# Self-attention scores on two halves of TensorE's rows, in units of two blocks

## The chip, the cores and the metric

The kernel runs on one core of one Trainium2 chip, as one program. The metric is the device time of one execution in microseconds. Engines are named as in the profile: PE is TensorE, DVE VectorE, ACT ScalarE, POOL GpSimd, SP SyncE (here it only issues transfers).

## The reference, cut to what matters

Everything is fp32. An adapter block with 8 heads comes first, then a transformer block: self-attention, cross-attention and a gated feed-forward, each behind a layer norm and each added to x. The change is in self-attention, with 4 batches, 512 tokens, width 160, 20 heads of 64:

```python
DIM, HEADS, DHEAD = 160, 20, 64
q = jnp.einsum('bne,ef->bnf', x, wq).reshape(B, N, HEADS, DHEAD).transpose(0, 2, 1, 3)
k = jnp.einsum('bme,ef->bmf', ctx, wk).reshape(B, M, HEADS, DHEAD).transpose(0, 2, 1, 3)
v = jnp.einsum('bme,ef->bmf', ctx, wv).reshape(B, M, HEADS, DHEAD).transpose(0, 2, 1, 3)
scores = jnp.einsum('bhnd,bhmd->bhnm', q, k) * DHEAD ** (-0.5)
attn = jax.nn.softmax(scores, axis=-1)
out = jnp.einsum('bhnm,bhmd->bhnd', attn, v)
x = jnp.einsum('bnf,fe->bne', out.transpose(0, 2, 1, 3).reshape(B, N, HEADS * DHEAD), wo) + bo + x
```

In self-attention x and ctx are both the layer norm of x.

## The kernel before

The program runs `adapter`, `selfattn`, `crossattn` and `feedfwd` one after the other. In each, every engine has a queue of its own, written out in program order, and the engines meet only through semaphores. The change is in `selfattn`, and in the helpers of `Norm` that it calls.

`selfattn` works on pairs of heads, ten to a batch, as a pair fills 128 rows with its 2 x 64 columns of q and k. fp32 values are split in two parts, a rounded one (fp32r, "hi") and the rest ("lo"), and products are made of the parts. A projection of q or k is four matmuls of 512 columns (L202 to L205), one of v eight of 256 columns (L210 to L213). ScalarE rounds the result (`round_part`, L509, L512) and copies v (L516), VectorE makes the rest (`rest`, L586, L590).

The scores of one head have only 64 rows. So SyncE (`stack`) moves the parts with eight transfers a pair: `q_stack` holds hi over lo of one head on 128 rows, `k_stack` the same k part twice. Two matmuls (L416, L417) then give (q_hi + q_lo)(k_hi + k_lo), a block of 128 queries x 512 keys.

The loop runs over the 80 blocks n of a batch (a head has four, a pair eight). In slot n each engine does, in this order:

- TensorE: the scores of block n + 10 (`LEAD`), the value products of block n - 2 (`LAG`) for both heads of a pair, every second slot (L446), four transposes of the probabilities (`turns`, L427), and where `step_at` says so a projection of a later pair.
- ScalarE: the exponential of block n + 10 with its sum (`exps`, L524), every fourth slot the copy of transposed probabilities (`copy_turned`, L535), then `round_part` and `copy_att` (L530).
- VectorE: the row maxima of block n + 10 (`maxima`, L595), the reciprocal of the sum (`inverses`, L600), `copy_turned` in the other three slots (L605), then `rest`.
- GpSimd: the scaling of the probabilities by the reciprocal (`scale`, L665).

The scores have two banks, the transposed blocks two, the value products two (`b_out`, used by the output projection L454 as well), the projections two. `probs` has room for four heads: the first exponential of a head waits until the transposes of the head four before it are done. The copies of transposed blocks go to four buffers. In a batch, statistics of the next layer norm are made at slot 37, and it is turned (L157, L161) at slot 57 (`TURN_AT`), on the banks of the projections.

Of the kernel before, what the change touches and what calls it, by code (L numbers as in the profile page):

```python
# [19 lines left out]
F32 = mybir.dt.float32  # L20
F32R = mybir.dt.float32r
# [75 lines left out]
class Norm:  # L97
# [53 lines left out]

    def turn(self, pe, b, ident, banks, bank_free):

        pe.wait_ge(self.s_hat.sem, self.s_hat.at(self.before + b, QT - 1))
        bank_free(0)
        for q in range(QT):
            last = pe.transpose(banks[0][:, q * P:(q + 1) * P], self.hat[:, q, 0:P], ident[:])  # L157
        last.then_inc(self.s_turned.sem, 1)
        bank_free(1)
        for q in range(QT):  # L160
            last = pe.transpose(banks[1][0:DT, q * P:(q + 1) * P], self.hat[:, q, P:D], ident[:])  # L161
        last.then_inc(self.s_turned.sem, 1)

    def scale(self, act, b, banks):
# [4 lines left out]
        act.activation(self.full[:], banks[0], ACT.Identity, bias=self.shift[:, 0:1], scale=self.gain[:, 0:1]).then_inc(self.s_full.sem, 1)  # L169
        act.wait_ge(self.s_turned.sem, self.s_turned.at(self.before + b, 1))  # L170
        act.activation(self.full_tail[:], banks[1][0:DT, :], ACT.Identity, bias=self.shift[0:DT, 1:2], scale=self.gain[0:DT, 1:2]).then_inc(self.s_full.sem, 1)
# [79 lines left out]
def selfattn(nc, x, ident, ln, next_ln, w_q, w_k, w_v, w_o, bias_o, banks, next_w_q, raw):  # L251

    LEAD, LAG = 10, 2  # L260
    NB = H1 * QT
    PAIRB = 2 * QT
    V_BUF = (0, 1, 2, 0, 1)
    V_BEFORE = (3 - 5, 4 - 5, 2 - 5, 0, 1)
    PS = 4
    TS = 4
    LN_AT = 37
    TURN_AT = (NPAIR - 3) * PAIRB + 1

    PROJECT, ROUND, REST = (20, 19, 16), (19, 18, 15), (18, 17)
    START = {1: (1, 0), 2: (1, 1), 3: (1, 2), 8: (2, 0), 9: (2, 1)}

    def step_at(n, ahead):

        for what, a in enumerate(ahead):
            j, off = divmod(n + a, PAIRB)
            if off == 0:
                return j, what  # L280
        return None

    def product_of(n):

        return n // 2

    with ExitStack() as ctx:
        sb = lambda n, s, d=F32: ctx.enter_context(nc.sbuf_tensor("sa_" + n, s, d))
        sig = lambda n, per, credit=0, step=1: Signal(ctx, nc, "sa_" + n, per, credit, step)
        q_stack = sb("q_stack", [P, 2, 2, S], F32R)  # L290
        k_stack = sb("k_stack", [P, 2, 2, 2, S], F32R)
        q_parts = sb("q_parts", [P, 2, S], F32R)
        k_parts = sb("k_parts", [P, 2, S], F32R)
        v = sb("v", [P, 3, QT, 2 * P])
        probs = sb("probs", [P, PS, QT, S])
        turned = sb("turned", [P, TS, S])
        att = sb("att", [P, NPAIR, S])
        negmax = sb("negmax", [P, 4 * QT])
        total = sb("total", [P, 4 * QT])
        inverse = sb("inverse", [P, 4 * QT])  # L300

        b_scores, b_turn, b_out, b_proj = banks[0:2], banks[2:4], banks[4:6], banks[6:8]
# [9 lines left out]

        s_stack = [sig(f"stacked{i}", NPAIR // 2, 0, 8 * 16) for i in range(2)]
        s_scores = sig("scores_made", NB, 8 * QT)
        s_max = sig("max_made", NB)
        s_exp = sig("exp_made", NB, 4 * QT)
        s_inv = sig("inverse_made", NB)
        s_norm = sig("probs_scaled", NB)
        s_noted = ctx.enter_context(nc.semaphore("sa_inverse_noted"))
        s_noted_sp = ctx.enter_context(nc.semaphore("sa_parts_noted"))  # L320
        s_turn = sig("turned_made", NB, 4 * QT)
        s_evac = sig("turned_copied", NB * 3 // 4, 3)
        s_evac_act = sig("turned_copied_act", NB // 4, 1)
        s_pv = sig("pv_made", NB // 2, 6 * QT)
        s_att = sig("att_copied", NPAIR, 2)
        s_o = sig("out_projected", 2, 2)
        s_bias = sig("bias_added", 1)
        s_x = sig("x_updated", QT, QT)
# [7 lines left out]
        def wait_turned_copied(eng, b, n):  # L336
            g, k = divmod(n, 4)
            if k == 3:
                eng.wait_ge(s_evac_act.sem, s_evac_act.at(b, g))
            else:  # L340
                eng.wait_ge(s_evac.sem, s_evac.at(b, 3 * g + k))
# [3 lines left out]
        @block.sync  # L345
        def _(sp):
            def stack(b, j):

                s = j % 2
                places = [(e, slice(e * HD, (e + 1) * HD), half, slice(half * HD, (half + 1) * HD)) for e in range(2) for half in range(2)]  # L350
                sp.wait_ge(s_scores.sem, s_scores.at(b, PAIRB * (j - 1) - 1))
                sp.sem_inc(s_noted_sp, 1)
                sp.wait_ge(s_qlo.sem, s_qlo.at(b, j))
                for e, rows, half, to in places:
                    sp.dma_start(q_stack[to, s, e, :].bitcast(F32), q_parts[rows, half, :].bitcast(F32)).then_inc(s_stack[s].sem, 16)
                sp.sem_inc(s_noted_sp, 1)
                sp.wait_ge(s_klo.sem, s_klo.at(b, j))
                for e, rows, half, to in places:
                    sp.dma_start(k_stack[to, s, e, :, :].bitcast(F32), k_parts[rows, :, :].bitcast(F32)).then_inc(s_stack[s].sem, 16)

            for j in range(3):
                stack(0, j)

            def batch(b, more):
                for j in range(3, NPAIR):
                    stack(b, j)
                if more:
                    for j in range(3):
                        stack(b + 1, j)
                else:  # L370
                    sp.wait_ge(s_q.sem, s_q.at(b, NPAIR - 1))
                    w_q.load(sp, next_w_q, raw, s_next)

            over_batches(sp, batch)

        @block.tensor
        def _(pe):
# [3 lines left out]
            def turn_norm(norm, b, nb):  # L381

                def bank_free(i):

                    if i == 0:
                        pe.wait_ge(s_vsb.sem, s_vsb.at(b, -1))
                    else:
                        pe.wait_ge(s_klo.sem, s_klo.at(b, -1))
                norm.turn(pe, nb, ident, b_proj, bank_free)

            def project(b, j, what):
                if j == 0 and what == 0:
                    ln.ready(pe, b)
                if what == 0:
                    if j > 0:
                        pe.wait_ge(s_vsb.sem, s_vsb.at(b, j - 1))
                    ln.project(pe, b_proj[0], w_q, j * P).then_inc(s_q.sem, 1)
                elif what == 1:
                    if j > 0:
                        pe.wait_ge(s_klo.sem, s_klo.at(b, j - 1))  # L400
                    ln.project(pe, b_proj[1], w_k, j * P).then_inc(s_k.sem, 1)
                else:
                    pe.wait_ge(s_qlo.sem, s_qlo.at(b, j))
                    for t in range(2):
                        last = ln.project_tokens(pe, b_proj[0][:, t * 2 * P:(t + 1) * 2 * P], w_v, j // 2 * 2 * P, j % 2 * 2 + t, 2 * P)
                    last.then_inc(s_v.sem, 1)

            def scores(b, n):
                h, q = divmod(n, QT)
                j, e = divmod(h, 2)  # L410
                if n % PAIRB == 0:
                    pe.wait_ge(s_stack[j % 2].sem, s_stack[j % 2].at(b, j // 2))
                pe.wait_ge(s_exp.sem, s_exp.at(b, n - 2))
                lhs = q_stack[:, j % 2, e, q * P:(q + 1) * P]
                bank = b_scores[n % 2]
                pe.matmul(bank, lhs, k_stack[:, j % 2, e, 0, :], start=True, stop=False)  # L416
                pe.matmul(bank, lhs, k_stack[:, j % 2, e, 1, :], start=False, stop=True).then_inc(s_scores.sem, 1)  # L417

            def turns(b, n):
                j, i = divmod(n, PAIRB)  # L420
                k, e = divmod(i, 2)
                h = 2 * j + e
                if k == 0:
                    pe.wait_ge(s_norm.sem, s_norm.at(b, QT * h + QT - 1))
                wait_turned_copied(pe, b, n - 2)
                for q in range(QT):
                    last = pe.transpose(b_turn[n % 2][:, q * P:(q + 1) * P], probs[:, h % PS, q, k * P:(k + 1) * P], ident[:])  # L427
                last.then_inc(s_turn.sem, 1)

            def pv(b, n):  # L430

                j, i = divmod(n, PAIRB)
                k, e = divmod(i, 2)
                if e == 0:
                    return
                wait_turned_copied(pe, b, n - 1)
                wait_turned_copied(pe, b, n)
                if k == 0:
                    pe.wait_ge(s_vsb.sem, s_vsb.at(b, j | 1))
                    if j >= 2:  # L440
                        pe.wait_ge(s_att.sem, s_att.at(b, j - 2))
# [1305 lines left out]
```

## Time and profile before

| | |
|---|---|
| runs (3) | median 1209.48 us, 1207.38 to 1214.39 |
| profiled execution | span 1209.3 us |
| TensorE busy | 1143.5 us, 95% |
| VectorE, ScalarE, GpSimd busy | 748.8, 621.4, 355.7 us |
| self-attention | from about 213 to 888 us |
| mean granted TensorE clock | 0.983 |

The time of the program is its span with a little around it. Self-attention is over half of it. An engine's idle time matters only where the engine sets the end, so the rows are to be read by stretch and not by the shares of the whole.

### The profile page before, as it was taken

To read this page: it belongs to the slowest core of one execution; us is meant where nothing else is said; L and a number is where in the kernel's file an instruction comes from. 1 tells how busy PE (TensorE), PEld (TensorE's weight loads), DVE (VectorE), ACT (ScalarE), POOL (GpSimd) and SP (SyncE) were. 2 spreads that over 40 slices of the span, in tenths; PEclk is the share of its full clock that TensorE was granted. 3 is DMA by queue.
4 is the path that set the end of the run, shared out by engine and by line. 5 is a ranking of instruction groups with operands and counts; after the bars stand their busy time and mean duration, and the time that the engine had idled before them with its cause. 6 is when DMAs were issued, how large, how long until landed. Compare 5 with 4: busy or idle time off the path is not lost. (4 is left out here: it accounts for less than half of the span.)

```text
span 1209.3 us, 21134 instructions
## 1 busy us (share of the span) xinstructions
PE 1143.5 (95%) x6348; PEld 766.6 (63%) x6348; DVE 748.8 (62%) x1758; ACT 621.4 (51%) x1370; POOL 355.7 (29%) x470
## 2 busy tenths in 40 slices
PE   7999999599999899999999999999989999999898
PEld 3555555456666666657566567666577778786787
DVE  4374574377777377774777775777637575757253
ACT  2543444356566366663565663656516464646242
POOL 2330321233433133432334332333213131312110
PEclk9999999799999999999999999999989999999899
DMA  6500000444444244444244443445120000000000
GB/s 167 114 1 1 0 1 1 104 105 105 106 105 105 56 105 106 111 99 107 58 111 107 95 108 81 111 103 118 42 55 2 1 0 0 0 1 1 1 22 22
DMA packets 43427, 76.69 MB, mean 63 GB/s; under 512 B 13316, under 2 KB 21444, under 8 KB 43332
## 3 DMA queue, kind: packets, MB, share of 16 engines
q1 hardware_dynamic: 43332, 75.54, 27.0%
q8 instruction: 46, 0.75, 0.3%
q14 instruction: 49, 0.40, 0.1%
HBM read 11.29 MB, written 1.31 MB: 10 GB/s over the span
## 5 line engine op out<-in xcount | busy, mean ns | idle before, releaser
L524 ACT ACTIVATE sa_probs<-banks,sa_negmax 128x512 f32<-128x512 f32 x320 | 220.9, 690 | 268.1 <-DVE sa_negmax L595 267.5
L665 POOL TENSOR_SCALAR sa_probs<-sa_probs,sa_inverse 128x512 f32<-128x512 f32 x320 | 223.1, 698 | 418.6 <-DVE sa_inverse L600 418.6
L595 DVE TENSOR_REDUCE sa_negmax<-banks 128x1 f32<-128x512 f32 x320 | 219.5, 686 | 104.8 <-PE banks L417 104.6
L427 PEld LDWEIGHTS banks<-ident,sa_probs 128*128 128x128 f32 x1280 | 146.5, 140 | 150.1 <-issue 69.1
L605 DVE COPY sa_turned<-banks 128x512 f32<-128x512 f32 x240 | 162.8, 679 | 66.4 <-PE banks L427 66.0
L427 PE MATMUL banks<-ident,sa_probs 128*128 128x128 f32 x1280 | 200.1, 279 | 1.1 <-issue 1.1
L446 PE MATMUL banks<-sa_turned,sa_v 128*64 128x512 f32 x640 | 172.6, 617 | 3.0 <-ACT sa_turned L535 1.7
L416 PE MATMUL banks<-sa_k_stack,sa_q_stack 128*128 128x512 f32 x320 | 144.8, 453 | 19.3 <-DMA sa_k_stack<-sa_k_parts 8.2
L417 PE MATMUL banks<-sa_k_stack,sa_q_stack 128*128 128x512 f32 x320 | 127.8, 399 | 0.0
L1537 POOL TENSOR_TENSOR ca_probs<-ca_probs,ca_inverse 128x616 f32<-128x616 f32 x40 | 48.8, 1219 | 162.4 <-DVE ca_inverse L1485 162.4
L416 PEld LDWEIGHTS banks<-sa_k_stack,sa_q_stack 128*128 128x128 f32 x320 | 61.3, 192 | 28.8 <-ACT sa_probs L524 13.6
L1417 ACT COPY ca_turned<-banks 77x512 f32<-77x512 f32 x80 | 42.7, 583 | 71.6 <-PE banks L1350 71.6
L446 PEld LDWEIGHTS banks<-sa_turned,sa_v 128*64 128x64 f32 x640 | 31.8, 134 | 59.7 <-issue 50.2
L1341 PEld LDWEIGHTS banks<-ca_k_diag,ca_q 128*128 128x128 f32 x320 | 45.3, 197 | 34.3 <-DVE ca_v L1466 23.2
L417 PEld LDWEIGHTS banks<-sa_k_stack,sa_q_stack 128*128 128x128 f32 x320 | 61.8, 193 | 3.6
L524 ACT ACTIVATION_READ_ACCUMULATOR sa_probs<-banks,sa_negmax 128x1 f32 x320 | 62.6, 196 | 0.0
L1341 PE MATMUL banks<-ca_k_diag,ca_q 128*128 128x154 f32 x320 | 54.0, 314 | 5.4 <-DVE ca_v L1466 2.8
L535 ACT COPY sa_turned<-banks 128x512 f32<-128x512 f32 x80 | 46.2, 577 | 8.2 <-PE banks L427 8.2
L600 DVE RECIPROCAL sa_inverse<-sa_total 128x1 f32<-128x1 f32 x320 | 49.0, 153 | 0.4 <-ACT sa_probs L524 0.4
L1360 PE MATMUL banks<-ca_turned,ca_v 77*64 77x512 f32 x160 | 46.1, 634 | 2.3 <-ACT ca_turned L1417 2.3
L1370 PEld LDWEIGHTS banks<-w_o,ca_att 128*128 128x128 f32 x320 | 45.7, 198 | 4.0 <-issue 4.0
L202 PE MATMUL banks<-ln_y_hi,wa_hi 128*128 128x512 f32 x80 | 39.3, 491 | 8.5 <-issue 3.5
(189 smaller groups left out, 1992.2 us busy)
## 6 DMA issues: line engine op xcount, KB each, us to landing
sa_k_stack<-sa_k_parts SPq DMA_DIRECT2D x160, 256.0 KB, 4.2
sa_q_stack<-sa_q_parts SPq DMA_DIRECT2D x160, 128.0 KB, 2.3
w_o<-in_L_xattn_wo SPq DMA_DIRECT2D x2, 800.0 KB, 6.3
out<-x SPq DMA_DIRECT2D x4, 320.0 KB, 2.5
x<-in_x SPq DMA_DIRECT2D x1, 960.0 KB, 5.3
ad_raw_main<-in_L_xattn_wq SPq DMA_DIRECT2D x1, 640.0 KB, 4.6
ad_raw_main<-in_L_xattn_wk SPq DMA_DIRECT2D x1, 640.0 KB, 7.4
ad_raw_main<-in_L_xattn_wv SPq DMA_DIRECT2D x1, 640.0 KB, 10.0
```

Of the source, the lines that this page charges most:

```text
L416: pe.matmul(bank, lhs, k_stack[:, j % 2, e, 0, :], start=True, stop=False)
L417: pe.matmul(bank, lhs, k_stack[:, j % 2, e, 1, :], start=False, stop=True).then_inc(s_scores.sem, 1)
L427: last = pe.transpose(b_turn[n % 2][:, q * P:(q + 1) * P], probs[:, h % PS, q, k * P:(k + 1) * P], ident[:])
L446: last = pe.matmul(b_out[j % 2][e * HD:(e + 1) * HD, :], v[:, V_BUF[j // 2], k, c:c + HD], turned[:, (n - 1 + e) % TS, :], start=(k == 0), ...
L524: act.activation(probs[:, h % PS, q, :], b_scores[n % 2], ACT.Exp, bias=negmax[:, c:c + 1], accum_out=total[:, c:c + 1]).then_inc(s_exp.se ...
L535: act.copy(turned[:, n % TS, :], b_turn[n % 2]).then_inc(s_evac_act.sem, 1)
L595: dve.tensor_reduce(negmax[:, c:c + 1], b_scores[n % 2], AX_X, ALU.max, negate=True).then_inc(s_max.sem, 1)
L600: dve.reciprocal(inverse[:, c:c + 1], total[:, c:c + 1]).then_inc(s_inv.sem, 1)
L605: dve.tensor_copy(turned[:, n % TS, :], b_turn[n % 2]).then_inc(s_evac.sem, 1)
L665: pool.tensor_scalar(probs[:, h % PS, q, :], probs[:, h % PS, q, :], inverse[:, c:c + 1], 1.0, ALU.mult, ALU.mult).then_inc(s_norm.sem, 1)
L1341: last = pe.matmul(b_scores[:, q // 2, (q % 2) * 2 * SK:(q % 2 + 1) * 2 * SK], q_sb[:, j % BUFS, q * P:(q + 1) * P], k_diag[:, j % BUFS, : ...
L1537: pool.tensor_tensor(p, p, inverse[:, j % BUFS, :].unsqueeze(2).broadcast_to([P, 2 * QT, SK]), ALU.mult).then_inc(s_norm.sem, 1)
```

## The change

The two heads of a pair are taken together. `q_parts` and `k_parts` now have two buffers and stay as they are, head 0 on rows 0 to 63, head 1 on rows 64 to 127; the stacks, their semaphores and SyncE's transfers go. The scores of a unit (block q of both heads) are six matmuls with 64 rows each: for hi x hi, lo x hi and hi x lo one of each head, into two banks. lo x lo is left out. The loop has 40 units a batch, LEAD is 5, and the value products of unit u - 1 follow the scores of unit u + 5. Each unit has eight transposes in two groups, one for each head, each with its bank. `probs` has room for two pairs, the copies of transposed blocks for two units. ScalarE copies head 1 of odd units, VectorE all others. Maxima and reciprocals are made for both heads in one instruction; exponentials and scalings stay one for each head. The projections have one bank, the value products one, and the output projection writes the banks of the transposes. `part_at` puts the projections of pair j + 2 behind units 4j, 4j + 1 and 4j + 2. The layer norm of what follows is turned in two steps, after units 23 and 27.

```diff
-    LEAD, LAG = 10, 2
-    NB = H1 * QT
-    PAIRB = 2 * QT
+    NU = NPAIR * QT
+    LEAD = 5
...
+    LN_AT = 12
+    TURN_MAIN, TURN_TAIL, ROUND_AT = 23, 27, 31
+    START = {0: (1, 0), 1: (1, 1), 2: (1, 2)}
+    def part_at(u):
+
+        j, what = u // QT + 2, u % QT
+        return (j, what) if what < 3 else None
...
-        q_stack = sb("q_stack", [P, 2, 2, S], F32R)
-        k_stack = sb("k_stack", [P, 2, 2, 2, S], F32R)
-        q_parts = sb("q_parts", [P, 2, S], F32R)
-        k_parts = sb("k_parts", [P, 2, S], F32R)
+        q_parts = sb("q_parts", [P, 2, 2, S], F32R)
+        k_parts = sb("k_parts", [P, 2, 2, S], F32R)
-        probs = sb("probs", [P, PS, QT, S])
-        turned = sb("turned", [P, TS, S])
+        probs = sb("probs", [P, 2, 2, QT, S])
+        turned = sb("turned", [P, 2, 2, S])
...
-        b_scores, b_turn, b_out, b_proj = banks[0:2], banks[2:4], banks[4:6], banks[6:8]
+        b_scores, b_turn, b_out, b_proj = [banks.pair(0), banks.pair(2)], banks[4:6], banks[6], banks[7]
...
                 elif what == 1:
-                    if j > 0:
-                        pe.wait_ge(s_klo.sem, s_klo.at(b, j - 1))
-                    ln.project(pe, b_proj[1], w_k, j * P).then_inc(s_k.sem, 1)
+                    pe.wait_ge(s_qlo.sem, s_qlo.at(b, j))
+                    ln.project(pe, b_proj, w_k, j * P).then_inc(s_k.sem, 1)
...
+            def scores(b, u):
+
+                j, q = divmod(u, QT)
+                if q == 0:
+                    pe.wait_ge(s_klo.sem, s_klo.at(b, j))
+                pe.wait_ge(s_exp.sem, s_exp.at(b, 2 * u - 3))
+                bank = b_scores[u % 2]
+                for i, (a, c) in enumerate(((0, 0), (1, 0), (0, 1))):
+                    for e in range(2):
+                        rows = slice(e * HD, (e + 1) * HD)
+                        last = pe.matmul(bank[:, e, :], q_parts[rows, j % 2, a, q * P:(q + 1) * P], k_parts[rows, j % 2, c, :],
+                                         start=(i == 0), stop=(i == 2))
+                last.then_inc(s_scores.sem, 1)
...
+            def turns(b, u):
+
+                j, k = divmod(u, QT)
                 if k == 0:
+                    pe.wait_ge(s_norm.sem, s_norm.at(b, 2 * QT * j + 2 * QT - 1))
+                for e in range(2):
...
+                    wait_turned_copied(pe, b, u - 1, e)
+                    for q in range(QT):
+                        last = pe.transpose(b_turn[e][:, q * P:(q + 1) * P], probs[:, j % 2, e, q, k * P:(k + 1) * P], ident[:])
+                    last.then_inc(s_turn.sem, 1)
...
+                for u in range(NU):
+                    m = u + LEAD
+                    if m < NU:
                         scores(b, m)
                     elif more:
+                        scores(b + 1, m - NU)
+                    if u >= 1:
+                        pv(b, u - 1)
+                    turns(b, u)
...
+                    if u == TURN_MAIN:
+                        norm.turn_main(pe, nb, ident, b_proj, lambda: pe.wait_ge(s_vsb.sem, s_vsb.at(b, u // QT + 2)))
...
+                wait_turned_copied(pe, b, NU - 1, 0)
+                pe.wait_ge(s_att.sem, s_att.at(b, NPAIR - 2))
+                project_out(0, 0, NPAIR - 2)
+                pv(b, NU - 1)
...
+            def exps(b, u):
+                j, q = divmod(u, QT)
+                act.wait_ge(s_max.sem, s_max.at(b, u))
                 if q == 0:
+                    act.wait_ge(s_turn.sem, s_turn.at(b, 2 * QT * (j - 1) - 1))
+                for e in range(2):
+                    act.activation(probs[:, j % 2, e, q, :], b_scores[u % 2][:, e, :], ACT.Exp, bias=negmax[:, u % RING, e:e + 1],
+                                   accum_out=total[:, u % RING, e:e + 1]).then_inc(s_exp.sem, 1)
...
+            def copy_turned(b, u):
+                act.wait_ge(s_turn.sem, s_turn.at(b, 2 * u + 1))
+                act.wait_ge(s_pv.sem, s_pv.at(b, u - 2))
+                act.copy(turned[:, u % 2, 1, :], b_turn[1]).then_inc(s_evac_act.sem, 1)
...
+                    if u % QT == 0 and u > 0:
+                        copy_att(b, u // QT - 1)
+                    if u % 2 == 1:
+                        copy_turned(b, u)
...
+            def maxima(b, u):
+                dve.wait_ge(s_scores.sem, s_scores.at(b, u))
+                dve.tensor_reduce(negmax[:, u % RING, :], b_scores[u % 2], AX_X, ALU.max, negate=True).then_inc(s_max.sem, 1)
...
+                    copy_turned(b, u, 0)
+                    if u % 2 == 0:
+                        copy_turned(b, u, 1)
```

## Rows read from the trace of the kernel before

**Rows 1.** The page: busy us, share of the span and instructions of each engine.

```profile
PE 1143.5 (95%) x6348; PEld 766.6 (63%) x6348; DVE 748.8 (62%) x1758; ACT 621.4 (51%) x1370; POOL 355.7 (29%) x470
```

**Rows 2.** Busy time by stretch: stretch, length, engines (instructions), granted clock, DMA share, GB/s.

```profile
310.28:325.61 15.33, 15.00 (x83) 9.14 (x82) 12.92 (x37) 8.49 (x21) 6.27 (x10) 1.00 0.46 105
325.61:340.30 14.69, 14.69 (x83) 9.09 (x82) 10.64 (x25) 9.53 (x25) 7.52 (x10) 1.00 0.47 108
340.30:357.32 17.02, 16.02 (x91) 9.91 (x89) 12.37 (x27) 11.76 (x28) 5.93 (x8) 1.00 0.42 98
...
386.71:416.50 29.79, 26.66 (x163) 20.09 (x162) 11.64 (x29) 9.84 (x24) 5.54 (x8) 1.00 0.26 60
```

**Rows 3.** Timeline of TensorE in steady state: start, length (us), engine, line, tiles.

```profile
428.21 0.48 PE L416 MATMUL banks<-sa_k_stack,sa_q_stack 128*128 128x512 f32 x1
428.53 0.40 PE L417 MATMUL banks<-sa_k_stack,sa_q_stack 128*128 128x512 f32 x1
428.86 1.08 PE L446 MATMUL banks<-sa_turned,sa_v 128*64 128x512 f32 x4
429.87 0.66 PE L427 MATMUL banks<-ident,sa_probs 128*128 128x128 f32 x4
430.28 0.47 PE L416 MATMUL banks<-sa_k_stack,sa_q_stack 128*128 128x512 f32 x1
430.60 0.40 PE L417 MATMUL banks<-sa_k_stack,sa_q_stack 128*128 128x512 f32 x1
430.83 0.60 PE L427 MATMUL banks<-ident,sa_probs 128*128 128x128 f32 x4
431.19 0.47 PE L202 MATMUL banks<-ln_y_hi,wa_hi 128*128 128x512 f32 x1
...
432.19 0.40 PE L416 MATMUL banks<-sa_k_stack,sa_q_stack 128*128 128x512 f32 x1
```

**Rows 4.** Timeline of all engines, the same stretch.

```profile
422.44 0.68 DVE L586 SCALAR_TENSOR_TENSOR sa_q_parts<-banks,sa_q_parts 128x512 fp32r<-128x512 f32 x1
...
423.04 0.68 DVE L595 TENSOR_REDUCE sa_negmax<-banks 128x1 f32<-128x512 f32 x1
...
425.56 0.40 PE L417 MATMUL banks<-sa_k_stack,sa_q_stack 128*128 128x512 f32 x1
...
426.00 0.69 DVE L595 TENSOR_REDUCE sa_negmax<-banks 128x1 f32<-128x512 f32 x1 [0.36 <-PE banks L417]
...
426.72 0.69 ACT L524 ACTIVATE sa_probs<-banks,sa_negmax 128x512 f32<-128x512 f32 x1 [0.94 <-DVE sa_negmax L595]
...
433.77 0.66 PE L427 MATMUL banks<-ident,sa_probs 128*128 128x128 f32 x4
...
434.27 0.59 ACT L509 ACTIVATE sa_q_parts<-banks 128x512 fp32r<-128x512 f32 x1
434.46 0.69 DVE L605 COPY sa_turned<-banks 128x512 f32<-128x512 f32 x1 [0.83 <-PE banks L427]
```

**Rows 5.** Timeline, ScalarE near the start of self-attention.

```profile
245.38 0.69 ACT L524 ACTIVATE sa_probs<-banks,sa_negmax 128x512 f32<-128x512 f32 x1 [1.36 <-DVE sa_negmax L595]
...
246.06 0.68 ACT L524 ACTIVATE sa_probs<-banks,sa_negmax 128x512 f32<-128x512 f32 x1
```

**Rows 6.** Timeline near the end of self-attention.

```profile
870.82 0.59 ACT L535 COPY sa_turned<-banks 128x512 f32<-128x512 f32 x1 [4.35 <-PE banks L427]
...
871.55 1.08 PE L446 MATMUL banks<-sa_turned,sa_v 128*64 128x512 f32 x4 [0.33 <-ACT sa_turned L535]
...
874.09 1.08 PE L446 MATMUL banks<-sa_turned,sa_v 128*64 128x512 f32 x4 [0.44 <-DVE sa_turned L605]
```

**Rows 7.** Timeline of the first scores; in brackets the idle time before.

```profile
226.31 0.79 PE L416 MATMUL banks<-sa_k_stack,sa_q_stack 128*128 128x512 f32 x1 [8.21 <-DMA sa_k_stack<-sa_k_parts]
```

**Rows 8.** Timeline of VectorE, the statistics of the next layer norm.

```profile
314.17 0.99 DVE L131 BATCH_NORM_STATS2 ln_stats<-x 128x6 f32 x4
...
315.61 0.66 DVE L595 TENSOR_REDUCE sa_negmax<-banks 128x1 f32<-128x512 f32 x1
```

More of the change, by code:

```diff
@@ L251, in selfattn @@
 def selfattn(nc, x, ident, ln, next_ln, w_q, w_k, w_v, w_o, bias_o, banks, next_w_q, raw):
-    LEAD, LAG = 10, 2
-    NB = H1 * QT
-    PAIRB = 2 * QT
+    NU = NPAIR * QT
+    LEAD = 5
     V_BUF = (0, 1, 2, 0, 1)
     V_BEFORE = (3 - 5, 4 - 5, 2 - 5, 0, 1)
[L265 to L285, printed above, removed]
+    RING = 8
+    LN_AT = 12
[4 more added lines that the diff above has]
+        return (j, what) if what < 3 else None
     with ExitStack() as ctx:
@@ L346, in _ @@
         def _(sp):
[L347 to L374, printed above, removed]
+            sp.wait_ge(s_q.sem, s_q.at(B - 1, NPAIR - 1))
+            w_q.load(sp, next_w_q, raw, s_next)
         @block.tensor
@@ L444, in pv, with project_out @@
                 for e in range(2):
                     c = j % 2 * P + e * HD
-                    last = pe.matmul(b_out[j % 2][e * HD:(e + 1) * HD, :], v[:, V_BUF[j // 2], k, c:c + HD],
-                                     turned[:, (n - 1 + e) % TS, :], start=(k == 0), stop=(k == QT - 1))
+                    last = pe.matmul(b_out[e * HD:(e + 1) * HD, :], v[:, V_BUF[j // 2], k, c:c + HD],
+                                     turned[:, u % 2, e, :], start=(k == 0), stop=(k == QT - 1))
                 last.then_inc(s_pv.sem, 1)
-            def project_out(b, q, first, end):
+            def project_out(q, first, end):
@@ L478, in batch @@
+                    if u == TURN_MAIN + 1:
+                        pe.wait_ge(norm.s_full.sem, norm.s_full.at(norm.before + nb, 0))
+                    if u == TURN_TAIL + 1:
+                        pe.wait_ge(norm.s_full.sem, norm.s_full.at(norm.before + nb, 1))
+                    if part_at(u):
+                        j, what = part_at(u)
                         if j < NPAIR:
@@ L616, in _ @@
             for what in range(2):
                 rest(0, 0, what)
-            for n in range(LEAD):
-                if n in START and START[n][1] < 2:
-                    rest(0, *START[n])
-                maxima(0, n)
-                if n >= 1:
-                    inverses(0, n - 1)
+            for u in range(LEAD):
+                maxima(0, u)
+                if u in START and START[u][1] < 2:
+                    rest(0, *START[u])
+                if u >= 1:
+                    inverses(0, u - 1)
@@ L625, in batch @@
             def batch(b, more):
[L626 to L628 removed]
+                for u in range(NU):
+                    m = u + LEAD
+                    if m < NU:
                         maxima(b, m)
                     elif more:
[L631 to L632 removed]
+                        maxima(b + 1, m - NU)
+                    if m - 1 < NU:
                         inverses(b, m - 1)
```

304 lines of the change are left out of this document (121 added, 183 removed).

## The prediction

> **What bounds the kernel now.** I read the page first: TensorE is busy 95% of the span, VectorE 62% [rows 1]. Then the busy times by stretch, cut at the starts of query projections, which come once per pair of heads in self-attention. In steady state a pair takes 14.69 us, all of it busy TensorE, at the full clock [rows 2]. Once per batch a pair takes 17.02 us (the next layer norm is turned there), once 15.33 us (its statistics sit in VectorE's queue). The third view is TensorE's timeline [rows 3], from which each step is priced by start to start. One pass over two blocks is 2.98 us (428.21 to 431.19): a scores matmul 0.235; the value products 1.01, and 0.10 more for the scores matmul before them (0.33 for 0.23); four transposes 0.41 and 0.36, and 0.08 more for the matmul behind each (0.32 for 0.235), so 0.49 and 0.44. Sum: 4 x 0.235 + 0.10 + 1.01 + 0.49 + 0.44 = 2.98. A projection of q or k is 1.00 less that 0.08, so 0.92; v is taken at 0.96. A pair: 4 x 2.98 + 2.80 = 14.72, the 14.69 measured. So here only TensorE's own work counts, as long as nothing it waits for is late. The rest of the argument is what becomes late.
>
> **TensorE's own work.** A unit (two blocks) had four scores matmuls on 128 rows. It gets six on 64 rows, in three couples on the two halves of the array. No row shows couples on row halves. The nearest are the value products, couples on column halves: one fp32 product of 512 columns would be four passes of about 0.22, 0.9 alone, and two of them take 1.01 together [rows 3]. So I take 0.235 a couple, 0.705 a unit; bounds 0.235 (free) and 0.47 (one after the other). Entering the row halves is a change the old order didn't have at this place (transposes led into plain matmuls). Price: below, nothing; above, 0.3 (three times the 0.10 that the change before the value products costs); I take 0.15, that 0.10 and a little for the second half starting later. New unit: 0.15 + 0.705 + 0.10 + 1.01 + 0.49 + 0.44 = 2.90, 0.085 less than before. Over 160 units: **-13.6**.
>
> The Trainium skill, page TensorEngine Tiling (Array Packing), Tiling Modes, says that changing the tiling mode drains TensorE. The trace agrees (the 0.10 above); if that rule cost nothing here the total would be 1229.6 us (worked below), with it 1237.
>
> **The wait that appears.** probs now holds two pairs. `exps(b, u)` with u = 4j, the first of pair j, waits for the last transposes of pair j-2, those of unit 4j-5. It stands in slot 4j-5 of ScalarE's queue, and the two exponentials stand ahead of `copy_turned` of that same slot, whose odd unit ScalarE copies. TensorE's value products of unit 4j-5 need that copy, and now come one slot later with only one scores unit between (no projection follows a unit with u % 4 = 3). Before, the wait was there too, but the copy was one block further on and the products two. The chain from the start of the second four transposes: they end and release in 0.63 (0.60 long [rows 3], and 0.03 as 433.77 + 0.66 to 434.46 [rows 4]); two exponentials at 0.68 [rows 5] = 1.36; copy and wake-up 0.73 (870.82 to 871.55 [rows 6]). Sum 2.72. TensorE fills 0.44 + 0.15 + 0.705 + 0.10 = 1.40 of it. It stands idle 1.32 us in every fourth unit: nine times a batch, eight in the last (the batch's last unit is followed by the output projection): 35 x 1.32 = **+46.2**. This stall doesn't shrink when the scores get cheaper.
>
> **A second chain.** q's rest on VectorE stands ahead of the next unit's maxima. From the start of q's projection: last matmul ends 0.705 + 0.40 later, wake-up 0.04 (425.56 to 426.00 is 0.44 [rows 4]), rounding 0.59, 0.03, then the maxima 0.60 behind the rest (422.44 to 423.04). The maxima of two blocks: between 0.69 and 1.38, taken at twice that spacing of 0.60, and 0.05 of wake-up, 1.25. Two exponentials 1.36, copy 0.73. Sum 5.71. TensorE's own way there: 0.92 + 0.15 + 0.705 + 0.10 + 1.01 + 0.49 + 0.44 + 0.92 + 0.15 + 0.705 + 0.10 = 5.69. Just hidden: **0**. If the change of mode were free it would cost 0.32. So a pair becomes 2.72 + 1.01 + 0.49 for the stalled unit, and 3 x 3.82 + 0.04 for the others: 15.7 us.
>
> **The rest.** All are small against the wait.
> - The last layer-norm turn: split over units 23 and 27, both stalled ones, with copies in ScalarE's slack. The 17.02 - 14.69 = 2.33 goes four times: **-9.3**.
> - Statistics: 1.44 on VectorE (314.17 to 315.61 [rows 8]) at unit 12, where q's rest already makes maxima late, so about 1.4 shows in place of 15.33 - 14.69 = 0.64: **+3**.
> - Start: the 8.21 wait for the stacking transfers [rows 7] goes, but one bank now makes k wait for q's rounding and rest (0.59 + 0.69), v for k's, and scores for v: 3.7 comes back: **-4.5**. Elsewhere the stacking transfers are hidden, so their removal is worth nothing; SyncE's queue has nothing behind them.
> - Batch end: the output projection now writes the transposes' banks and first waits for VectorE's copy (0.69 + 0.69 + 0.14 = 1.52 after the transposes begin, against 0.93): 0.6 x 4 = **+2.4**. A batch end costs 29.79 [rows 2]; its other waits I leave as they are.
> - Last batch, no scores or projections left to cover: a unit was 2.54 (871.55 to 874.09 [rows 6]). Now with the copy between: 0.63 + 0.73 + 1.01 + 0.49 = 2.86 when ScalarE copies, 0.28 more when VectorE makes both copies (0.69 + 0.60 + 0.83 from the first transposes). 0.45 x 5, and 1.2 for the three units before: **+3.5**.
> - VectorE's merged maxima and reciprocals, GpSimd's scales, one att bank, one update per half: VectorE was 72% busy in the steady pair (10.64 of 14.69), so nothing.
>
> Sum: -13.6 + 46.2 - 9.3 + 3 - 4.5 + 2.4 + 3.5 = +27.7. The profiled execution has a span of 1209.3 and the median of the runs is 1209.48, the same within 0.2. Forecast **1237.0**.
>
> Bounds by the unknown price of entering the row halves. At 0: own work -37.6, wait 35 x 1.47 = +51.6, second chain 35 x 0.32 = +11.2, rest the same: +20.3, 1229.6. At 0.3: +10.4, +41.1, 0: +46.6, 1256. The other terms may be off by some 8 together. Own range 1222 to 1262.
>
> **Rivals.**
> - *The other side: the chain over ScalarE doesn't hold TensorE.* If the copy of the odd unit is there when TensorE comes to it, the 46.2 goes and the total is 1209.3 - 18.5 = 1191. It decides at a stall of under 0.35 per fourth unit, where the total passes below 1203.4. For it: TensorE never waited for this copy in the steady pair before. Against it: the order of the queue and four durations, each from a row. Chance 0.11.
> - *Part of it:* stall of a third to two thirds, 1203 to 1222. Chance 0.10.
> - Forecast, 1222 to 1262: chance 0.60.
>
> 0.5% (6 us) is about what a measurement of this kernel can tell from no change. Under 1203.4: the third rival and a little of the part case, 0.13; within 6 us: 0.08; slower: 0.79. The range that leaves out the serial rival and the third one is 1205 to 1285.
>
> **What would show it.** In the profile after, query projections 15.7 apart in steady state. TensorE idle about 1.3 us before the value products of every fourth unit, released by ScalarE's copy into turned, and that copy right behind two exponentials that were released by transposes. TensorE's busy share falls to about 90%. The six scores matmuls start in couples, and the value products follow the first couple by some 0.8; if 1.5, the couples are serial. No 8 us wait at the start. Wrong would be a steady pair under 15 us, or one whose idle time stands before the scores (then the exponentials or maxima are the bound, which I take to be hidden).

## The result and the profile after

| | before | after |
|---|---|---|
| median (4 runs each, side by side) | 1208.84 us | 1242.13 us |
| range | 1207.38 to 1214.39 | 1241.65 to 1246.96 |
| span of the profiled execution | 1209.3 us | 1239.8 us |
| self-attention, first projection to the next stage's first | 677.3 us (213.42 to 890.72) | 706.9 us (215.82 to 922.76) |

The ratio is 1.0278 (95% interval 1.0229 to 1.0326): slower. Of the 30.5 us more in the span, 29.6 are in self-attention. The rest is outside it: the stage is reached 2.4 us later, and what follows it is 1.5 us shorter.

The page after: busy time of the engines, which answers to [rows 1], then costly groups.

```profile
PE 1140.1 (92%) x6668; PEld 742.7 (60%) x6668; DVE 730.4 (59%) x1430; ACT 611.1 (49%) x1370; POOL 351.9 (28%) x470
...
L485 ACT ACTIVATE sa_probs<-banks,sa_negmax 128x512 f32<-128x512 f32 x320 | 217.2, 684 | 272.7 <-DVE sa_negmax L557 206.4
...
L557 DVE TENSOR_REDUCE sa_negmax<-banks 128x2 f32<-128x1024 f32 x160 | 194.9, 1218 | 52.9 <-PE banks L371 50.3
L398 PE MATMUL banks<-sa_turned,sa_v 128*64 128x512 f32 x640 | 172.6, 617 | 47.3 <-ACT sa_turned L496 44.1
...
L371 PE MATMUL banks<-sa_k_parts,sa_q_parts 64*128 64x512 f32 x960 | 156.0, 430 | 4.4 <-issue 2.7
```

TensorE is busy 3 us less, 92% of the span instead of 95%. The group of the value products (L398) carries the new idle time, 47.3 us, nearly all of it ended by ScalarE's copy into turned (L496). The scores (L371) hardly wait: 4.4 us.

TensorE's waits for those products: us in total, times, longest.

```profile
PE banks L398 <- ACT sa_turned L496: 44.1, 43, 1.3
...
PE banks L398 <- DVE sa_turned L566: 3.1, 3, 1.0
```

Busy time by stretch, in the columns of [rows 2]: the pair with the statistics, a pair with a layer-norm turn, a plain pair.

```profile
290.69:307.71 17.02, 14.69 (x91) 8.44 (x90) 12.49 (x29) 8.83 (x23) 6.79 (x11) 1.00 0.00 0
323.44:339.17 15.73, 15.05 (x95) 8.87 (x94) 10.23 (x17) 9.03 (x22) 5.09 (x8) 1.00 0.01 2
431.46:447.20 15.74, 14.62 (x91) 8.45 (x90) 10.21 (x17) 8.80 (x23) 5.47 (x8) 1.00 0.00 1
```

A plain pair is 15.74 (15.71 to 15.74 in the first three batches, mean 15.72; 15.87 to 15.89 in the last) where it was 14.69. The pair with the turn has 15.05 of busy TensorE in 15.73, so the turn sits in idle time; before it took 17.02 [rows 2].

Timeline of one stalled unit after, TensorE and ScalarE.

```profile
442.23 1.10 PE L385 MATMUL banks<-ident,sa_probs 128*128 128x128 f32 x8
...
443.26 0.96 PE L371 MATMUL banks<-sa_k_parts,sa_q_parts 64*128 64x512 f32 x6
443.37 0.69 ACT L485 ACTIVATE sa_probs<-banks,sa_negmax 128x512 f32<-128x512 f32 x1 [1.89 <-PE banks L385]
...
444.05 0.68 ACT L485 ACTIVATE sa_probs<-banks,sa_negmax 128x512 f32<-128x512 f32 x1
...
444.71 0.58 ACT L496 COPY sa_turned<-banks 128x512 f32<-128x512 f32 x1
...
445.34 1.08 PE L398 MATMUL banks<-sa_turned,sa_v 128*64 128x512 f32 x4 [1.12 <-ACT sa_turned L496]
...
446.35 1.09 PE L385 MATMUL banks<-ident,sa_probs 128*128 128x128 f32 x8
...
447.20 0.47 PE L218 MATMUL banks<-ln_y_hi,wa_hi 128*128 128x512 f32 x1
```

The reader is to follow ScalarE. Transposes end and release the exponential at 443.37. It needed their place in probs, and ScalarE had stood idle for 1.89 before it. Two exponentials run, and only then the copy at 444.71, whose transposed blocks had been ready as long as the exponential had. TensorE has done its six scores matmuls and stands 1.12 before the value products, which start as soon as the copy ends.

### The profile page after: what moved, and what is told of

It reads as the page before. It is cut to its first block and busy times, and to the rows that moved or that the text cites. A ratio compares the mean times of both kernels' runs of the same rounds, so it can differ in the third digit from the quotient of the medians.

```text
span 1239.8 us, 20399 instructions
## 1 busy us (share of the span) xinstructions
PE 1140.1 (92%) x6668; PEld 742.7 (60%) x6668; DVE 730.4 (59%) x1430; ACT 611.1 (49%) x1370; POOL 351.9 (28%) x470
## 5 line engine op out<-in xcount | busy, mean ns | idle before, releaser
L557 DVE TENSOR_REDUCE sa_negmax<-banks 128x2 f32<-128x1024 f32 x160 | 194.9, 1218 | 52.9 <-PE banks L371 50.3
L398 PE MATMUL banks<-sa_turned,sa_v 128*64 128x512 f32 x640 | 172.6, 617 | 47.3 <-ACT sa_turned L496 44.1
L385 PEld LDWEIGHTS banks<-ident,sa_probs 128*128 128x128 f32 x1280 | 137.9, 141 | 129.1 <-issue 125.1
L566 DVE COPY sa_turned<-banks 128x512 f32<-128x512 f32 x240 | 157.3, 683 | 72.6 <-PE banks L385 71.9
L385 PE MATMUL banks<-ident,sa_probs 128*128 128x128 f32 x1280 | 175.7, 280 | 1.0 <-POOL sa_probs L626 1.0
L371 PE MATMUL banks<-sa_k_parts,sa_q_parts 64*128 64x512 f32 x960 | 156.0, 430 | 4.4 <-issue 2.7
L371 PEld LDWEIGHTS banks<-sa_k_parts,sa_q_parts 64*128 64x128 f32 x960 | 79.0, 187 | 54.1 <-issue 32.3
L398 PEld LDWEIGHTS banks<-sa_turned,sa_v 128*64 128x64 f32 x640 | 32.1, 134 | 106.9 <-ACT sa_turned L496 54.4
L553 DVE TENSOR_TENSOR sa_k_parts<-banks,sa_k_parts 128x512 fp32r<-128x512 f32 x40 | 27.7, 692 | 70.8 <-ACT sa_k_parts L473 70.8
L1302 PEld LDWEIGHTS banks<-ca_k_diag,ca_q 128*128 128x128 f32 x320 | 44.1, 192 | 34.6 <-DVE ca_v L1427 23.3
L496 ACT COPY sa_turned<-banks 128x512 f32<-128x512 f32 x80 | 46.7, 584 | 10.8 <-PE banks L385 10.8
L1331 PEld LDWEIGHTS banks<-w_o,ca_att 128*128 128x128 f32 x320 | 46.2, 199 | 4.0 <-issue 4.0
L405 PEld LDWEIGHTS banks<-w_o,sa_att 128*128 128x128 f32 x320 | 43.7, 190 | 5.8 <-issue 3.2
L1331 PE MATMUL banks<-w_o,ca_att 128*128 128x160 f32 x320 | 47.2, 311 | 0.0
L405 PE MATMUL banks<-w_o,sa_att 128*128 128x160 f32 x320 | 45.6, 302 | 1.6 <-DVE sa_turned L566 1.6
```

The lines of the kernel that those rows point to most:

```text
L371: last = pe.matmul(bank[:, e, :], q_parts[rows, j % 2, a, q * P:(q + 1) * P], k_parts[rows, j % 2, c, :], start=(i == 0), stop=(i == 2))
L385: last = pe.transpose(b_turn[e][:, q * P:(q + 1) * P], probs[:, j % 2, e, q, k * P:(k + 1) * P], ident[:])
L398: last = pe.matmul(b_out[e * HD:(e + 1) * HD, :], v[:, V_BUF[j // 2], k, c:c + HD], turned[:, u % 2, e, :], start=(k == 0), stop=(k == QT ...
L405: last = pe.matmul(b_turn[q // 2][:, q % 2 * D:(q % 2 + 1) * D], att[:, j, q * P:(q + 1) * P], w_o[:, j, :], start=(j == 0), stop=(j == NP ...
L496: act.copy(turned[:, u % 2, 1, :], b_turn[1]).then_inc(s_evac_act.sem, 1)
L557: dve.tensor_reduce(negmax[:, u % RING, :], b_scores[u % 2], AX_X, ALU.max, negate=True).then_inc(s_max.sem, 1)
```

## The experiments

All pair times are start to start of query projections. Times of the stage, self-attention, are from its first projection to the next stage's first, in the profiled execution. The first four kernels start from the changed kernel, the next three (head_by_head, dummy_transfers, statistics_moved) from copy_first, the last three from statistics_moved.

**1. The copy ahead of the exponentials, in the fourth unit alone.**

```diff
+                    if u % QT == 3:
+                        copy_turned(b, u)
                     (the exponentials of unit u + LEAD)
...
-                    if u % 2 == 1:
+                    if u % QT == 1:
```

> In every unit with u % 4 = 3, ScalarE copies the transposed block before its two exponentials, not after. Theory (the exponentials that wait for the same unit's transposes hold the copy): the 1.12 us idle before the value products of each fourth unit goes, a steady pair falls from 15.72 to 14.6 us, and the total by 36 x 1.12 = 40 to about 1202, some 0.6% under the kernel before. Rival (scores on row halves and their change of mode are what costs, the idle time only moves): the pair stays above 15.3 and the total above 1225.

Measured: 1206.52 us beside 1210.24 before, ratio 0.9959 (0.9937 to 0.9980). The span falls from 1239.8 to 1208.6. The same unit in its timeline:

```profile
437.33 1.10 PE L385 MATMUL banks<-ident,sa_probs 128*128 128x128 f32 x8
...
438.35 0.96 PE L371 MATMUL banks<-sa_k_parts,sa_q_parts 64*128 64x512 f32 x6
438.53 0.59 ACT L496 COPY sa_turned<-banks 128x512 f32<-128x512 f32 x1 [1.92 <-PE banks L385]
439.02 0.69 ACT L485 ACTIVATE sa_probs<-banks,sa_negmax 128x512 f32<-128x512 f32 x1
...
439.25 1.08 PE L398 MATMUL banks<-sa_turned,sa_v 128*64 128x512 f32 x4
```

The copy now starts 1.20 after the transposes begin and not 2.48, the exponentials wait behind it, and the value products follow the scores with no idle time. From the transposes to the value products it is 1.92 where it was 3.11 (442.23 to 445.34). So the place of one instruction in a queue held all of the loss and more: the theory stands. Two stretches of it, a plain pair and the one with the statistics:

```profile
277.81:292.36 14.55, 14.55 (x92) 8.45 (x90) 10.18 (x17) 8.70 (x23) 5.47 (x9) 1.00 0.01 2
292.36:308.25 15.89, 14.61 (x91) 8.43 (x90) 12.50 (x29) 8.69 (x23) 6.66 (x11) 1.00 0.00 0
```

The pair is 14.55, all TensorE. What the idle time had hidden comes back: 14.97 in the two pairs with a turn, 15.69 in the pair with the layer norm's remainder (two subtractions on VectorE). That is why the total is 1206.5 and not the 1202 expected: the stage is 34.6 us shorter (706.9 to 672.4), not 40, as 8 x 0.42 + 3 x 1.14 = 6.8 us reappear.

**2. ScalarE copies head 1 of even units instead of odd ones.** No copy of ScalarE then stands in the slot of the late exponentials.

```diff
-                    if u % 2 == 1:
+                    if u % 2 == 0:
                         copy_turned(b, u)
```

> ScalarE copies head 1 of even units, VectorE all other blocks. Theory: in the fourth unit VectorE does both copies and the products wait 0.3 instead of 1.12; but in the unit behind which v is projected the copy comes after late exponentials, 0.4 of new idle time. A pair 15.25, the total down by 17 to about 1225. Rival (any copy there is as late, since TensorE is simply ahead): no change, 1242.

Measured: 1224.84, ratio 1.0098 (1.0070 to 1.0127). Plain pairs are 14.88 to 14.90, those with a turn 15.11 and 15.33, those with the statistics or the remainder about 16.3. The 44.1 us of waits for ScalarE's copy fall to 14.5 in 29 waits, and 6.3 in 7 come for VectorE's, which now makes both copies of odd units one after the other. This is between the two orders. The total is the one expected, but the sizes are not: in a plain pair the two waits are 0.14 for VectorE (expected 0.3) and 0.27 for ScalarE (expected 0.4), which is better than the 15.25 forecast for a pair, and the pairs with other work, up to 16.30, make up for it.

**3 and 4. Two products and four products instead of three.** The first leaves hi x lo out of the scores, the second adds lo x lo.

```diff
-                for i, (a, c) in enumerate(((0, 0), (1, 0), (0, 1))):
+                for i, (a, c) in enumerate(((0, 0), (1, 0))):
```

```diff
+                for i, (a, c) in enumerate(((0, 0), (1, 0), (0, 1), (1, 1))):
```

> The product hi x lo is left out of the scores (two couples of matmuls a unit, not three). Theory (two chains over VectorE and ScalarE bound the units they end in): only one of the four units of a pair gets shorter by the full 0.23, a pair 15.5, span down by some 9 us. Rival (TensorE's own work bounds all units): 0.23 x 160 = 37 us less.

> The product lo x lo is added (four couples a unit). Theory: the stalled unit takes the couple into its idle time, the other three grow by 0.235, a pair 16.4, span up by about 29 us. Rival (couples one after the other, or every unit bound by TensorE): 0.235 x 160 = 38 us or, if serial, 75.

Measured, one execution each: spans 1231.2 (8.6 less) and 1268.8 (29.0 more). The spans aren't clean, since in both a few us of the stage ran at a lower granted clock (0.83 from 634 to 644 with two products, 0.79 from 417 to 425 and 0.69 from 598 to 609 with four). The plain pairs, all at 1.00, are 15.31 to 15.39 and 16.43, beside 15.72. A couple is 0.235 in each of four units, 0.94 a pair. Adding it costs 0.71, three times 0.235: the stalled unit takes it for nothing. Taking it away gives back 0.33 to 0.41 only, and the waits for the copy grow from 44.1 to 64.3 us. That is the sign of a chain over another engine: less work on TensorE mostly makes its idle time longer.

**5. The six matmuls in the order of heads**, all three of head 0 and then all three of head 1.

```diff
-                for i, (a, c) in enumerate(((0, 0), (1, 0), (0, 1))):
-                    for e in range(2):
+                for e in range(2):
+                    for i, (a, c) in enumerate(((0, 0), (1, 0), (0, 1))):
```

> The kernel with the copy first (span 1208.6 us, steady pair 14.55 us, TensorE never idle in it), and in each unit the three products of head 0 come before the three of head 1. Theory (the couples share the array's time, and TensorE keeps its order): only the third product of head 0 and the first of head 1 overlap, five steps of 0.235 in place of three, 0.47 more in every unit, a pair 16.4, span up by 75 us. Rival (the two row halves don't overlap in either order, 0.15 a matmul is what 64 rows cost): no change.

Measured, one execution: 1207.64, span 1205.6, pair 14.57. Nothing is lost, and the expectation fails. The rival on record, no overlap in either order, gives the same number. The start times within one unit, in ns, of the changed kernel and of this one, are both in couples:

```
couples in program order:   432574 432577 | 432908 432911 | 433144 433147
head by head:               432706 432716 | 433043 433053 | 433279 433289
```

The records don't name the rows, so which matmul is which is inferred. Two of the same half don't start together (0.23 to 0.34 apart in experiment 9, which also rules out the rival), so each couple here must be one of each half: TensorE starts matmuls of the free row half past those that wait for the busy one. The order in the program doesn't matter here.

**6. Eight dummy transfers a pair**, as large as the stacking ones, waited for by nobody but SyncE and its counting.

> The kernel with the copy first, and SyncE issues for each pair eight transfers of the old sizes and shapes, from the output weights to tiles that nobody reads. Theory (the stacking transfers were hidden in steady state, and share nothing with the engines that sets the end): no change, 1206.5, a pair 14.55. Rival (they took bandwidth from the engines' reads): some 0.1 us or more a pair, 1211 or above.

Measured: 1206.79, ratio 0.9964 (0.9939 to 0.9988), pair 14.55. A stretch of it:

```profile
430.00:446.00 16.00, 16.00 (x98) 8.79 (x94) 11.12 (x18) 9.47 (x25) 5.90 (x9) 1.00 0.52 118
```

DMA is at 0.52 and 118 GB/s, as in the same window of the kernel before (0.52, 120), and TensorE is never idle. The transfers that the change removes were hidden in steady state. At the start of self-attention they weren't, there TensorE waited for the first ones [rows 7].

**7. The statistics moved** from slot 12 to 14, and the two steps that follow them from 14 and 16 to 18 and 20.

```diff
-    LN_AT = 12
+    LN_AT = 14
...
-                    if u == LN_AT + 2:
+                    if u == LN_AT + 4:
...
-                    if more and u == LN_AT + 4:
+                    if more and u == LN_AT + 6:
```

> The kernel with the copy first, and the statistics and the standardizing of the next layer norm move from units 12 and 14 to units 14 and 18, both behind VectorE's copies where no rest of q or k is made, and where ScalarE's exponentials wait for transposes anyway. Theory: the pair with the statistics falls from 15.9 to 14.6, four times, so 5 us less: 1201. Rival (1.4 us of VectorE work shows wherever it stands): no change.

Measured: 1197.65 (1196.14 to 1201.17) beside 1210.97 before, ratio 0.9898 (0.9879 to 0.9916). The pair that was 15.89 and the one with the remainder:

```profile
284.90:299.46 14.56, 14.56 (x91) 8.45 (x90) 11.24 (x25) 8.71 (x23) 6.16 (x10) 1.00 0.00 0
358.50:374.19 15.69, 14.70 (x92) 8.48 (x90) 10.86 (x19) 9.19 (x23) 5.71 (x9) 1.00 0.00 0
```

The pair with the statistics takes no longer than a plain one now, and the stage is 5.5 us shorter than in copy_first (666.9 for 672.4), the 5 expected. The medians differ by 8.9. The rest isn't this edit's doing as far as the traces show: outside the stage the two kernels are the same, and the profiled executions had a mean granted clock of 0.987 here and 0.979 in copy_first. This version beats both kernels, the one before by 1.0% and the changed one by some 3.7% (0.9898 against 1.0278).

**8. The remainder on GpSimd**, in slot 30.

```diff
+                    if u == ROUND_AT - 1:
...
+                        pool.tensor_tensor(norm.lo[:], norm.full[:], norm.hi[:].bitcast(F32), ALU.subtract).then_inc(norm.s_lo.sem, 1)
```

> The kernel before this one (statistics moved), and the two subtractions of the next layer norm go from VectorE (unit 31) to GpSimd (unit 30). Theory: they hold VectorE's maxima of the next unit, and the pair of 15.68 falls to 14.6, four times: 4.4 us less than with the statistics moved alone, about 1197. Rival: the projection of the next batch waits for the rounding itself, and GpSimd's two operations are slower: no gain or a loss of 1 or 2 us.

Measured: 1201.32, ratio 0.9913 (0.9885 to 0.9940): no gain. The last pair falls to 14.55, but the one before it rises to 15.89. The timeline of GpSimd, and TensorE's transposes behind it:

```profile
362.03 1.27 POOL L656 TENSOR_TENSOR ln_y_lo<-ln_full,ln_y_hi 128x512 fp32r<-128x512 f32 x1 [0.93 <-ACT ln_y_hi L193]
363.45 1.27 POOL L659 TENSOR_TENSOR ln_y_tail<-ln_full_tail,ln_y_tail 32x512 fp32r<-32x512 f32 x1 [0.16 <-POOL ln_y_lo L656]
365.01 2.69 POOL L626 TENSOR_SCALAR sa_probs<-sa_probs,sa_inverse 128x512 f32<-128x512 f32 x4 [0.28 <-POOL ln_y_tail L659]
...
366.42 1.09 PE L385 MATMUL banks<-ident,sa_probs 128*128 128x128 f32 x8 [1.27 <-POOL sa_probs L626]
```

Two subtractions of 1.27 each make the scaling of a pair's last unit (35) late, and the pair's first transposes, which need all four units scaled, wait 1.27 for it. The number is the rival's. Of its reasons the slower operations hold, but what waits for them are the transposes and not the next batch's projection.

**9. All six matmuls on rows 0 to 63.** Both heads' scores are made from head 0's rows, so only the time is of use.

```diff
-                        rows = slice(e * HD, (e + 1) * HD)
+                        rows = slice(0, HD)
```

> The kernel with the copy first and the statistics moved, and the scores of head 1 are made from head 0's rows, so that all six matmuls lie on rows 0 to 63 and the output is not the reference's. Theory (what makes three couples cheap is that the two halves of the array work at once; the head-by-head order changed nothing because TensorE lets the halves run on independently): six steps of 0.235 in each unit, 0.70 more, a pair 17.4, span up by 113 us to about 1308. Rival (64 rows are simply faster, some 0.12 us a matmul wherever they lie): no change, 1195.

Measured, one execution: 1308.89, span 1306.9, pair 17.27, which is 2.72 more than 14.55 (0.68 a unit for the 0.70 expected). TensorE's timeline:

```profile
450.20 1.65 PE L371 MATMUL banks<-sa_k_parts,sa_q_parts 64*128 64x512 f32 x6
451.78 1.08 PE L398 MATMUL banks<-sa_turned,sa_v 128*64 128x512 f32 x4
452.79 1.09 PE L385 MATMUL banks<-ident,sa_probs 128*128 128x128 f32 x8
453.82 1.65 PE L371 MATMUL banks<-sa_k_parts,sa_q_parts 64*128 64x512 f32 x6
```

From the scores to the value products 1.58 (450.20 to 451.78), where it is 0.90: three steps of 0.23 more. A matmul on 64 rows takes as long (0.23) as one on 128 did [rows 3], and the couples are cheap only because the two halves run together.

**10. The remainder split over two slots of VectorE**, its first subtraction in slot 30, the second in 31.

```diff
+                    if u == ROUND_AT - 1:
...
+                        dve.tensor_tensor(norm.lo[:], norm.full[:], norm.hi[:].bitcast(F32), ALU.subtract).then_inc(norm.s_lo.sem, 1)
```

> The kernel with the copy first and the statistics moved, and the first of the next layer norm's two subtractions goes to the end of VectorE's unit 30, into the gap before the copy of unit 31, the second stays at unit 31. Theory: about 0.7 of the 1.13 us that the pair at unit 32 has over the others goes, four times, 1195 against 1197.7 for the kernel with both at unit 31. Rival (as on GpSimd: the earlier place holds something else): no change or a loss.

Measured: 1198.95, ratio 0.9910 (0.9877 to 0.9942): no gain. The two pairs are 15.39 and 14.78, 30.17 in place of 14.55 + 15.69 = 30.24. The rival holds: the first subtraction, at 358.93, makes VectorE's next maxima and its copy behind them late, and TensorE waits 0.45 for that copy (361.55) and 0.25 for the scalings (362.87).

## Why the prediction was right, step by step

Forecast 1237.0 (1205 to 1285, slower 0.79); measured 1242.13, and +30.5 of span, +29.6 of it in self-attention, against +27.7. The mechanism named is the one that copy_first removes. That the sum is so close is in part luck: own work was 8 us too favourable, and the wait (4 us) and the batch ends (about 1 us each) were too dear. The terms:

- **The wait that appears**, +46.2 = 35 x 1.32. Start to start a plain pair loses 15.72 - 14.55 = 1.17, by the order of the copy alone, and in the last batch 15.87 - 14.57 = 1.30; 27 x 1.17 + 8 x 1.30 = +42. The chain from the first of the eight transposes was put at 0.49 + 2.72 = 3.21 and is 3.11. The exponential starts 1.14 after them (1.12 taken), both take 1.34 (1.36), copy and wake-up 0.63 (0.73). TensorE's way meanwhile is 1.92 (1.89 taken). The 0.73 was read in the last batch of the kernel before [rows 6], and there it holds after as well: 819.43 to 820.16 below, where it is 0.64 in the stalled units of the first three batches. A price from one stretch was used for another.
- **Own work**, -13.6. This was mis-sized: 14.55 against 14.69 is 0.14 a pair, 40 x 0.14 = -5.6. A couple costs the 0.235 taken. Entering the row halves costs more. In the steady state after (timeline of TensorE below), the first couple starts 0.33 after the projection before it (432.24 to 432.57), 0.10 over 0.235, and scores take 0.89 to the value products (432.57 to 433.46), 0.08 over 0.705 + 0.10. That is 0.18 where 0.15 was taken; 4 x 0.03 = 0.12 a pair is 4.8 us of the 8 missing. Most of the rest is in my sums: 14.72 for the old pair's 14.69, and 14.52 with the measured price for the new one's 14.55, 0.06 x 40 = 2.4. The errors of this term (+8) and of the one above (-4) cancel by half.

```profile
432.24 0.40 PE L221 MATMUL banks<-ln_y_tail,wa_tail 96*128 96x512 f32 x1
432.57 0.96 PE L371 MATMUL banks<-sa_k_parts,sa_q_parts 64*128 64x512 f32 x6
433.46 1.08 PE L398 MATMUL banks<-sa_turned,sa_v 128*64 128x512 f32 x4
```

- **A second chain**, 0. No idle time stands before the value products of the other units, in the plain pairs after and in copy_first: hidden, as said.
- **The layer-norm turn**, -9.3: hidden as said (15.73 and 15.72 in the two pairs). That the cover was the stall shows when it is gone: 0.42 in each of two pairs, and 1.14 for the remainder.
- **Statistics**, +3 = 4 x (1.4 - 0.64). The pair went to 17.02, 1.30 above a plain one. The rows:

```profile
293.15 0.99 DVE L131 BATCH_NORM_STATS2 ln_stats<-x 128x6 f32 x4
...
294.59 1.19 DVE L557 TENSOR_REDUCE sa_negmax<-banks 128x2 f32<-128x1024 f32 x1
...
297.79 1.08 PE L398 MATMUL banks<-sa_turned,sa_v 128*64 128x512 f32 x4 [1.16 <-ACT sa_turned L496]
...
305.85 1.08 PE L398 MATMUL banks<-sa_turned,sa_v 128*64 128x512 f32 x4 [1.17 <-ACT sa_turned L496]
```

VectorE is held from 293.15, its maxima come at 294.59, and the value products at 297.79 wait 1.16 for the copy behind late exponentials, the usual stall at 305.85 coming on top. As the term said, 1.3 for 0.64: +2.6.

- **Start**, -4.5. The 8.21 wait [rows 7] is gone, and the two that replace it stand in TensorE's timeline:

```profile
215.82 0.47 PE L218 MATMUL banks<-ln_y_hi,wa_hi 128*128 128x512 f32 x1 [3.43 <-ACTq L459]
...
218.41 0.80 PE L218 MATMUL banks<-ln_y_hi,wb_hi 128*128 128x512 f32 x1 [1.41 <-DVE sa_q_parts L549]
...
221.89 0.58 PE L226 MATMUL banks<-wc_hi,ln_y_hi 128*128 128x256 f32 x1 [1.40 <-DVE sa_k_parts L553]
...
223.89 1.65 PE L371 MATMUL banks<-sa_k_parts,sa_q_parts 64*128 64x512 f32 x6
```

First scores come 8.07 after the first projection, before 12.89 (213.42 to 226.31): -4.8. The granted clock was low in both stretches (0.57 and 0.63), so the projections in them took longer than in steady state.

- **Batch end and last batch**, +2.4 and +3.5. By start to start of output projections:

| stretch | before | after | more | terms say |
|---|---|---|---|---|
| start to the first | 180.25 | 182.82 | +2.6 | +3.0 |
| first to second | 164.96 | 172.21 | +7.3 | +7.5 |
| second to third | 165.04 | 171.80 | +6.8 | +7.5 |
| third to fourth | 151.92 | 164.95 | +13.0 | +9.7 |

(7.5 is -3.4 + 11.9 - 2.3 + 0.75 + 0.6 a batch, 9.7 the same with one stall fewer and the 3.5.) The first three stretches look right only because errors cancel. In each, own work is 2.0 worse than the term (-1.4 for -3.4) and the wait 1.4 better (9 x 1.17 = 10.5 for 11.9). For the second and third that leaves -0.2 and -0.7 for a batch end, where +0.6 was taken. The wait before the output projection is there (0.43 at 398.64 after), but the 0.74 for ScalarE's probabilities at 412.25 before has no counterpart. In the last stretch the wait is as forecast (8 x 1.30 for 8 x 1.32), and own work shows. One of its stalled units:

```profile
818.09 0.69 ACT L485 ACTIVATE sa_probs<-banks,sa_negmax 128x512 f32<-128x512 f32 x1 [1.93 <-PE banks L385]
...
819.43 0.58 ACT L496 COPY sa_turned<-banks 128x512 f32<-128x512 f32 x1
...
820.16 1.08 PE L398 MATMUL banks<-sa_turned,sa_v 128*64 128x512 f32 x4 [1.27 <-ACT sa_turned L496]
```

The end of this stretch, without scores or projections:

```profile
890.04 1.08 PE L398 MATMUL banks<-sa_turned,sa_v 128*64 128x512 f32 x4 [0.27 <-ACT sa_turned L496]
...
893.18 1.08 PE L398 MATMUL banks<-sa_turned,sa_v 128*64 128x512 f32 x4 [1.03 <-DVE sa_turned L566]
...
896.05 1.08 PE L398 MATMUL banks<-sa_turned,sa_v 128*64 128x512 f32 x4 [0.77 <-ACT sa_turned L496]
...
899.14 1.08 PE L398 MATMUL banks<-sa_turned,sa_v 128*64 128x512 f32 x4 [0.99 <-DVE sa_turned L566]
...
902.01 1.08 PE L398 MATMUL banks<-sa_turned,sa_v 128*64 128x512 f32 x4 [0.77 <-ACT sa_turned L496]
...
905.15 1.08 PE L398 MATMUL banks<-sa_turned,sa_v 128*64 128x512 f32 x4 [1.04 <-DVE sa_turned L566]
...
907.60 0.68 PE L405 MATMUL banks<-w_o,sa_att 128*128 128x160 f32 x3 [0.35 <-DVE sa_turned L566]
```

And two lines of the kernel before:

```profile
861.65 1.08 PE L446 MATMUL banks<-sa_turned,sa_v 128*64 128x512 f32 x4
...
875.59 1.25 PE L454 MATMUL banks<-w_o,sa_att 128*128 128x160 f32 x8
```

A unit at the end of the last batch is 3.02 (890.04 to 905.15, five of them), as the 2.86 and 3.14 of the prediction say. Before it was 2.49 (861.65 to 874.09) and not the 2.54 read from one of them: 0.53 for the 0.45 taken. And the output projection comes 2.45 after the last value products listed, before 1.50 (874.09 to 875.59), 0.95 for 0.6. With the 2.0 of own work this makes 2.8 of the 3.3 us more than the terms say; about half a microsecond stays unassigned. The stalled units of this batch also have 1.27 idle and not 1.12, 0.09 of it between copy and products and 0.06 between transposes and exponentials. Why both are longer here I didn't test.

One sum of the recorded bounds is off: 35 x 1.47 is 51.5, not 51.6. Nothing hangs on it.

The rival of the other side, that the chain doesn't hold TensorE, falls with 44.1 us in 43 waits, and the one of a part of it with 1.12 to 1.27 of idle time in each stalled unit where no turn fills it. The rivals of serial couples and of half an overlap fall with 14.55 in copy_first against 17.27 in same_half, where the couples are serial. The Trainium skill, page TensorEngine Tiling (Array Packing), Tiling Modes, says that a change of tiling mode drains TensorE. The trace agrees that a change costs time, though not why: 0.10 into the row halves and 0.08 more out of them, 0.18 a unit, by which the case without it (1229.6) falls.

## What to carry to other kernels

When a buffer gets smaller or a slot larger, go through each in-order queue and ask what stands behind the instruction that now waits, and who needs it: here an exponential with nothing to hurry for held a copy that TensorE needed, and putting that copy first in one slot of four turned +2.8% into -0.4%. Idle time created in one place hides other work; when it is mended, look at once for what comes back (here statistics, turns and remainder; moving the first took 5.5 us out of the stage, two attempts at the last gained nothing). A kernel that gains little when work is taken from its busiest engine is held by a chain over another one in part of its units: here a couple more cost three quarters of its price, a couple less gave back under a half. And a price is to be read in the stretch where it will be used: the 0.73 for copy and wake-up held in the last batch alone.

## What the runs showed that I had not expected

- Six matmuls on two row halves take the same time in both program orders (0.90 to the next products; pair 14.55 and 14.57): by the inference in experiment 5, one half's matmuls start past those queued for the other. I had expected +75 us for the order by heads.
- The starts of a couple are 3 ns apart (10 ns in the order by heads).
- A subtraction of 128x512 takes GpSimd 1.27 us (362.03), and one of 32x512 the same 1.27.
